# Two more states turned on ScalarE, two more products on GpSimd, a fourth scaled buffer and a later copy in a selective-scan kernel

## The reference

```python
A = -jnp.exp(A_log)
dbc = jnp.einsum('bld,nd->bln', x, x_proj_w)
delta, Bm, Cm = jnp.split(dbc, [DT_RANK, DT_RANK + D_STATE], axis=-1)
delta = jax.nn.softplus(jnp.einsum('blr,dr->bld', delta, dt_proj_w) + dt_proj_b)
deltaA = jnp.exp(delta[..., None] * A)
BX = delta[..., None] * Bm[:, :, None, :] * x[..., None]
# h[t] = deltaA[t] * h[t-1] + BX[t]
y = jnp.einsum('blds,bls->bld', hs, Cm)
return y + Dp * x
```

## Time and profile before

| | us |
|---|---|
| median of three executions | 3326.68 |
| the profiled execution's own time | 3325.57 |
| its span in the trace | 3323.8 |
| DVE busy | 3116.9 (94%) |
| GpSimd (POOL) busy | 3008.9 (91%) |
| ScalarE (ACT) busy | 2867.6 (86%) |
| TensorE (PE) busy | 2553.0 (77%) |
| GpSimd, product with B, L474: 640 of 2390 ns | 1514.9 |
| GpSimd, product with C, L462: 416 of 2379 ns | 984.1 |

### The profile page before, as it was taken

How to read it: one execution, slowest core, us unless ns; L and a number is a source line. 1 busy time by engine, 2 the same in 40 slices (tenths; PEclk the granted TensorE clock), 3 DMA queues, 4 the chain that set the end, 5 groups by cost and what they waited for, 6 DMA issues and landing times. The chain is left out here.

```text
span 3323.8 us, 47833 instructions
## 1 busy us (share of the span) xinstructions
PE 2553.0 (77%) x15542; PEld 2043.0 (61%) x15542; DVE 3116.9 (94%) x2059; ACT 2867.6 (86%) x5338; POOL 3008.9 (91%) x1422
## 2 busy tenths in 40 slices
PE   7777777877778777777777778777777777877776
PEld 5566556666556666566666566666666665666665
DVE  3899999999999999999999999999999999999999
ACT  4889888889888889888888888898889888888985
POOL 2889999989999989999989999989999989999997
PEclk9998999998999988999988999988999888999888
DMA  5433334433244433344433444433444333344331
GB/s 156 144 123 116 108 120 123 126 119 118 97 132 124 128 118 112 106 125 128 126 110 108 126 119 128 119 112 100 131 125 129 118 105 114 122 126 126 107 115 51
DMA packets 273358, 394.09 MB, mean 119 GB/s; under 512 B 45003, under 2 KB 119508, under 8 KB 273108
## 3 DMA queue, kind: packets, MB, share of 16 engines
q1 hardware_dynamic: 273108, 391.03, 38.9%
HBM read 348.98 MB, written 25.18 MB: 113 GB/s over the span
## 5 line engine op out<-in xcount | busy, mean ns | idle before, releaser
L474 POOL TENSOR_TENSOR bx<-dx,b_sb 128x1024 f32<-128x1024 f32 x640 | 1514.9, 2390 | 53.9 <-DVE hs L849 53.7
L849 DVE TENSOR_TENSOR_SCAN hs<-decay,bx 128x1024 f32<-128x1024 f32 x640 | 1456.1, 2280 | 40.1 <-issue 15.9
L1079 PE MATMUL y<-ident,hc 128*128 128x128 f32 x8192 | 1134.1, 289 | 61.2 <-DVE hc L827 36.8
L1079 PEld LDWEIGHTS y<-ident,hc 128*128 128x128 f32 x8192 | 1015.0, 150 | 183.4 <-DVE hc L827 91.5
L462 POOL TENSOR_TENSOR hc<-hs,c_sb 128x1024 f32<-128x1024 f32 x416 | 984.1, 2379 | 11.1 <-DVE hs L849 11.1
L849 DVE TENSOR_TENSOR_SCAN hs<-decay_sb,decay 128x1024 f32<-128x1024 f32 x384 | 864.5, 2272 | 44.1 <-ACT decay_sb L744 38.4
L744 ACT ACTIVATE decay<-delta,rate 128x512 f32<-128x512 f32 (+1 forms) x1280 | 824.5, 682 | 39.3 <-DVE hs L849 38.9
L827 DVE TENSOR_TENSOR hc<-hs,c 128x1024 f32<-128x1024 f32 x608 | 728.5, 1198 | 34.2 <-PE c L1062 25.1
L585 ACT ACTIVATE dxb<-dxT,btok 128x256 f32<-128x256 f32 x1536 | 651.0, 497 | 0.0
L1054 PE MATMUL decay<-ident,dxb 128*128 128x128 f32 x3072 | 443.7, 292 | 228.1 <-DVE hs L849 219.4
L1054 PEld LDWEIGHTS decay<-ident,dxb 128*128 128x128 f32 x3072 | 367.5, 149 | 338.1 <-issue 250.0
(11 more groups left out here) (126 smaller groups left out, 2324.5 us busy)
## 6 DMA issues: line engine op xcount, KB each, us to landing
b_sb<-b_scratch SPq DMA_DIRECT2D x640, 256.0 KB, 3.2
c_sb<-b_scratch SPq DMA_DIRECT2D x416, 256.0 KB, 3.6
xin<-in_L_attn_x_dram SPq DMA_DIRECT2D x32, 512.0 KB, 5.7
w_sb<-in_L_ffn_W_dram SPq DMA_DIRECT2D x32, 512.0 KB, 3.9
w2o_sb<-w2o_scratch SPq DMA_DIRECT2D x32, 512.0 KB
xres<-in_L_attn_x_dram SPq DMA_DIRECT2D x32, 512.0 KB, 5.3
out_dram<-og SPq DMA_DIRECT2D x32, 512.0 KB, 4.3
dbc<-high SPq DMA_DIRECT2D x64, 128.0 KB, 2.3
```

What stands on the lines that cost most here:

```text
L474: nc.gpsimd.tensor_tensor(bx[:, i % RING, :, :], dx[:, g, :, :], b_sb[:, i % BRING, :].unsqueeze(1).broadcast_to([P, DT, T]), ALU.mult).th ...
L849: V.tensor_tensor_scan(hs[:, s % HSLOTS, :, :].rearrange("p k t -> p (k t)")[:, u], factor.rearrange("p k t -> p (k t)")[:, u], data.rearr ...
L1079: ins = M(yps[:, c, k * P:(k + 1) * P], hc[:, s % RING, k, c * P:(c + 1) * P], ident[:, :], start=False, stop=(s == ADDED[-1]), is_transpo ...
```

## The change

States 12 and 26 go from `POOL_B` to `TURNED`; the scaling of state 26 stands at ScalarE's step 21. As the entries of `SCALED_AT` belong to the entries of `TURNED` in order, the scalings of states 12, 13, 14 and 15 stand at steps 7, 8, 9 and 11, where those of 13, 14 and 15 stood at 7, 9 and 10. States 8 and 22 go from `ON_DVE` to `POOL_C`. The ring of B rows has five slots (`BRING`), and the scaled buffers are four (`XSLOTS`). The forward dx copies stand at ScalarE's steps 31 and 32, that is at step 31 of the row before and at step 0 of the row itself. The last hunk keeps the copy at step 32 out of row 0, whose forward copies are made before the loop.

```diff
--- before.py
+++ after.py
@@ -31,8 +31,8 @@
     RING = 4
     DSLOTS = 2
     HSLOTS = 4
-    BRING, CRING, C_AHEAD = 6, 5, 3
-    TSLOTS, XSLOTS = 2, 3
+    BRING, CRING, C_AHEAD = 5, 5, 3
+    TSLOTS, XSLOTS = 2, 4
 
     MEAN, SCALE, SHIFT, NORM = 0, 1, 4, 6
     TRANS, XNT, PROJECT, HIGH, LOW = (6, 7), (8, 9), (8, 9), 11, 12
@@ -40,16 +40,16 @@
     EXPAND, ABS = (14, 15, 24, 25), (16, 17, 26, 27)
     EXP, LN, SQUARE, RATIO = (18, 27), (19, 28), (20, 29), (21, 30)
     LOG1P, STEPSIZE, DX = (25, 36), (27, 39), (28, 43)
-    DX_TURN, DX_COPY = (28, 29, 44, 45), (30, 31, 46, 47)
+    DX_TURN, DX_COPY = (28, 29, 44, 45), (31, 32, 46, 47)
     FFN_IN, HIDDEN, GELU = (16, 16, 18, 18, 20, 20, 22, 22), (18, 20, 22, 24), 31
     FFN_OUT, GATE = (31, 31, 32, 32, 34, 34, 35, 35), (35, 38)
     FFN_OUT_FIRST, GATE_FIRST = (33, 33, 34, 34, 36, 36, 37, 37), (36, 38)
     Y_OUT, Y_RESIDUAL = 1, 5
     SKIP = {0: ((0, 0), (2, 0)), 1: ((0, 1), (1, 0), (1, 1), (2, 1)), 4: ((3, 0), (3, 1))}
 
-    TURNED, SCALED_AT, TURN_LEAD = (5, 6, 8, 9, 11, 13, 14, 15, 22, 24, 28, 30), (1, 2, 3, 4, 5, 7, 9, 10, 17, 19, 23, 25), 3
+    TURNED, SCALED_AT, TURN_LEAD = (5, 6, 8, 9, 11, 12, 13, 14, 15, 22, 24, 26, 28, 30), (1, 2, 3, 4, 5, 7, 8, 9, 11, 17, 19, 21, 23, 25), 3
     POOL_B = [s for s in range(STEPS) if s not in TURNED]
-    POOL_C, C_LAG, ADD_LAG = (2, 4, 5, 7, 9, 10, 11, 12, 16, 18, 20, 26, 27), 4, 2
+    POOL_C, C_LAG, ADD_LAG = (2, 4, 5, 7, 8, 9, 10, 11, 12, 16, 18, 20, 22, 26, 27), 4, 2
     ON_DVE = [s for s in range(STEPS) if s not in POOL_C]
     NT, NBX, ND, NPC = len(TURNED), len(POOL_B), len(ON_DVE), len(POOL_C)
     ADDED = [s for i in range(STEPS + ADD_LAG) for s in ((i - ADD_LAG,) if i - ADD_LAG in POOL_C else ()) + ((i,) if i in ON_DVE else ())]
@@ -637,7 +637,7 @@
                     high_part(row)
                 if s == B_COPY:
                     copy_btok(row, par)
-                if s in DX_COPY:
+                if s in DX_COPY and (row or s in DX_COPY[DT:]):
                     copy_dxT(row, DX_COPY.index(s))
                 if s in ABS:
                     absolute(row, par, ABS.index(s))
```

## The result

The changed kernel takes 3339.53 us (median of six executions, 3337.78 to 3343.57); the kernel before, measured beside it, 3327.03 us. The ratio is 1.0039, with a 95% interval of 1.0028 to 1.0050: slower, by more than the 0.2% that can be told from no change. I had predicted 3316 us, 10.5 us faster; it came out 12.5 us slower, inside the wide range of 3272 to 3348 us, outside the forecast's own of 3303 to 3329, and on the other side of no change. The profiled execution took 3338.66 us, with a span of 3336.9 us.

A forecast was written before the change was run, and what follows sets the result against it. No engine alone was taken as the bound, but a ring of engines waiting on each other. Terms -15.5, +18.2, -14.0, +3 and -2.2 gave -10.5 us, so 3316 us; own range 3303 to 3329, wide range 3272 to 3348.

The forecast's parts named there:

- GpSimd at no cost: GpSimd swaps B products 12 and 26 for C products 8 and 22 in the same places: cost 0.
- Later copies, -0.5 us: Start of row: ScalarE is free earlier, decay 2 no longer holds scan 2; half a microsecond a row, -15.5 us.
- First half: Scans 11 and 12 wait for decays behind ScalarE's added scaling: +0.8 us in slower rows, +0.2 in faster, +18.2 us.
- Second half: Scan 24 comes 0.17 us later, scan 26 1.05 us earlier in 15 slower rows: -14.0 us in all.
- Step 24, +3 us: One more TensorE addition (product 22) ahead of the delta unit makes decay 28 0.1 us late: +3 us over the rows.
- second rival: Slower: TensorE at 1.2 GHz at step 24 delays decay 28, 2.5 us a row in 15 rows; 3352 us, chance 0.18.
- The last row, -2.2: The last row has no front work on ScalarE, so its two products taken from DVE give -2.2 us.
- The first rival: DVE gets both products' time, 73 us or perhaps half: 3253 to 3290 us, put at 3275; chance 0.20.
- The sum: All terms over the whole kernel added: -10.5 us, giving a predicted 3316 us.
- The third rival: Nothing moves: gains at scans 2 and 26 return as waits at scans 3, 28 or `zz`; 3326 us, chance 0.17.

The follow-up runs named there:

- b2: Kernel after with the scalings of states 13 and 14 at steps 9 and 10 instead of 8 and 9: 3313.77 us, 0.9957.
- b3: Kernel after with state 12's four scalings writing one column of 256 each (its input is wrong): 3313.65 us, 0.9962.
- a1: Kernel before with only the forward dx copies one step later: 3285.42 us, 0.9873.
- a2: Kernel before with only state 12 turned, product 8 on GpSimd, four scaled buffers and five B slots: 3344.31 us, 1.0054.
- a3: Kernel before with only state 26 turned and product 22 on GpSimd, rings and copies as before: 3329.61 us, 1.0007.
- b4: Kernel after with state 26's four scalings writing one column each (its input is wrong): 3312.15 us, 0.9950.
- d1: Kernel after with TensorE's transposes of state 26 ahead of the C broadcast at step 23: 3364.64 us, 1.0110.
- c1: Kernel before with the later dx copies, state 12 turned, product 8 on GpSimd and the larger rings: 3332.32 us, 1.0017.
- d3: Kernel after with scalings 13 and 14 at steps 9 and 10, TensorE's transposes first at steps 3, 6, 19, 21, 23, 25: 3365.91 us, 1.0118.

## Why the prediction was wrong

Point by point, in the order of its steps; per row and against before:

- *GpSimd at no cost*: right, 3008.9 us busy in both, and scan 12's wait for it gone.
- *Later copies, -0.5 us*: right in its mechanism (scan 2 no longer waits), mis-sized. Alone it is -1.31; in the kernel after, 31-2 and 2-8 fall by 0.68 together, 21 us over 31 rows. I counted the one wait that it removes, and not what an earlier row start does to `zz` and to the stretch around step 24.
- *First half*: the waits at scans 11 and 12 came nearly as counted (0.94 and 0.54, forecast 1.3 and 0.6). Another of 0.56 at scan 10 was not counted. Missed altogether: TensorE waits 1.3 us for the xnT that scaling 13 delays, and in one row of four it then projects at the lower level (1.74 us for a pair; 1.02 at 1949.69 in the same row), hands `high` over 1.45 us late, and scans 13 and 14 are late too. The forecast gave +18.2 us; 8-15 rose by 0.86, which is 27 over 31 rows. Without the one kind of row that the lower level lengthens it rose by 0.45, which would be 14. b2 and b3 show this part: both take the 20.94 us rows away, and the waits of 0.94 and 0.54 or their equals stay.
- *Second half*: 22-24 came out at 6.79 (forecast 6.8), scan 26 without a wait, 24-26 at 6.63. The term of -14.0 us measured -10 (22-24 and 24-26 together, -0.33 x 31). The wait that it takes away stood at scan 26 in 12 rows, not in 15: three of the 15 waits for a PSUM decay are at the first scans of the kernel.
- *Step 24, +3 us*: this is the step that failed. 26-29 rose by 0.66, 20 us over 31 rows. The +3 us was 0.1 a row for one more addition with TensorE at the full level, and the rows in which the granted clock is 1.00 there show just that (7.80 or 7.81 against 7.70). But in half of the rows the lower level falls on the queue, and they take 8.50 and 9.37 us: the mechanism of the second rival, with the two additions at 2.69 us in the long row, where the forecast had 1.76 and that rival 3.4. I had argued that the removed wait of 2.92 us keeps TensorE at 2.4 GHz through steps 21 to 24. The wait was moved, not removed: it stands now at step 23, 2.88 us in front of the broadcast for state 24, with the queue of step 24 directly behind it. The Trainium skill's rule ("TensorE: Matmul & The Clock Gate", section "HAM oscillation — how this bites in real kernels") is that a gap in TensorE's work takes its clock to half, and it speaks of longer gaps than this one. The trace agrees with it in two kinds of row (0.62 and 0.81 of the clock over nine microseconds) and not in a third, where the granted clock is 1.00 behind the same gap. I had used the rule for the full level, without asking where the gap would stand afterwards.
- *The last row, -2.2*: -3.5 (95.09 us to 91.57 from the last row's L820 to the final one).
- *The first rival*, DVE getting its products' time, fell at the waits of scans 11, 12 and 24, which are there in every row looked at.
- *The sum*: added by place, the measured terms give the result: -21 (31-2 and 2-8), +27, -10, +20 and -3.5 are +12.5 us, and +12.5 were measured. The forecast had -15.5, +18.2, -14.0, +3 and -2.2. So the adding of places was sound, and step 24 makes 17 of the 23 us by which the forecast missed. What doesn't add is the parts, each run alone: -1.31 + 0.64 + 0.12 a row against +0.53. The medians of a1, a2 and a3 stand -41.5, +17.4 and +2.7 us to before; added that gives 3305, and 34 us more were measured.

As an estimate, the rows that the lower level lengthens in 8-15 (0.39 us a row) and in 26-29 (0.56) make 29 us over 31 rows, more than twice the 12.5 us that the change costs. It is a count from the table and the four kinds of row, not a measurement: in b2, b3 and b4 a stretch that got shorter was in part paid for elsewhere.

The second rival's form was right (slower, from step 24) and its price too high: 2.5 us in 15 rows, 1.2 a row, against 0.66. Its sign, a wait of over 1 us at scan 28, is there in one row of four (1.43), and a smaller one (0.57) in another. The third rival (3326 us) had the gain at scan 26 come back as a wait at scan 28, and that it did in these rows, but it had no loss in 8-15.

**What stays open.** The same gap stands in front of the same work in three kinds of row of the kernel after, and the low level covers most of that work in one, some in another and none in the third. The rows repeat in fours, threes or twos, so it isn't chance. That it depends on what earlier rows did is likely from this, but not shown, and no run here shows by what the chip decides it. So I can say which stretch the low level makes longer, and not forecast in how many rows. It wasn't tried to keep TensorE busy over the gap with matmuls that nobody needs; such a run would be the direct test of what the lower level costs.

## What to carry to other kernels

In a ring of engines with fixed orders, a part's price holds only for the kernel it was measured in: run the parts alone and in pairs before combining them, and ship the one that wins (here the later copies alone, 41 us faster, where the whole change is 12.5 us slower). Work moved to an engine that isn't the busiest still costs where that engine feeds a third one; ask who waits for the instruction behind it. When a wait goes, look where the same gap stands afterwards, and what is queued behind it.

## What the hardware showed that I had not expected

- Two gaps of TensorE of 1.85 and 1.94 us with 2.4 us of matmuls between them were followed by the low level in each row (d1). One gap of 2.88 us was followed by it in two kinds of row and not in a third, with the same work behind it (kernel after).
- Eight matmuls of one shape take 1.04 us and 1.92 us 42 us apart (kernel after), and the rows settle into cycles of two (100.27, 101.11 in b2), three (99.64, 101.29, 102.86 in c1) and four, or into none (102.40 in d1 and d3), by edits that don't change the amount of work.
- Work left out can lengthen another stretch by more than half of what it brings: b4 saves 0.85 us in 22-24 and pays 0.53 in 8-15.
